# Feed-forward by whole batches, and ternary weights by sign, in a two-layer decoder kernel

## Chip, cores and metric

The kernel runs on one core of one Trainium2 chip. The metric is the device time of one execution in microseconds. Engine names are those of the profile: PE is TensorE, PEld its weight load, DVE VectorE, ACT ScalarE, POOL GpSimd, SP SyncE.

## What is computed

Two decoder layers over x of shape (8, 128, 256), 8 batches of 128 tokens: attention, a causal convolution over a context, a ternary feed-forward, a selective scan, an fp8 cross attention, a mixture of experts. The change touches the end of the convolution and the feed-forward, whose reference is, cut to what matters:

```python
def activation_quant(x):
    s = 127 / clip(max(abs(x), axis=-1), 1e-5)
    return clip(round(x * s), -128, 127) / s
def weight_quant(w):
    s = 1.0 / clip(mean(abs(w)), 1e-5)
    return clip(round(w * s), -1, 1) / s
def bit_linear(x, w): return activation_quant(x) @ weight_quant(w).T
def rms_norm(x, weight): return weight * x * rsqrt(mean(x * x) + 1e-6)

x = x + ffn(layernorm(x))
ffn(x) = bit_linear(rms_norm(silu(bit_linear(x, w_gate)) * bit_linear(x, w_up)), w_down)
```

w_gate and w_up are 1024 x 256, w_down is 256 x 1024.

## The kernel before

Each engine has one instruction stream, written out by hand stage by stage: begin, attention, convolution, feed-forward (`ffn`), scan, cross attention, experts. Semaphores alone tie the streams, and each engine runs its own in order. A batch is a tile of 128 tokens on the partitions. `link` makes DVE or POOL wait for its own last instruction.

**Convolution** (L570). A loop of 16 turns, one for each head group h. POOL forms a product (L657) that waits for PE's turn before last, PE multiplies it by a Toeplitz matrix (L717 to L719, three matmuls of 512 columns in f32), DVE multiplies the result by the query (L674) and sums it (L676). Beside this loop, ACT makes the ternary weights in three pieces of 128 x 2048: it takes the mean of their magnitude (L700), then scales and adds a constant that rounds (L706) and subtracts it (L707). In turns 10, 11 and 12, DVE clamps a rounded piece to -1..1 (L680). POOL ends with two centrings of later weights (L1329, from L660). ACT squares other weights (L1309, L1313, called from L709); the last four wait for those centrings. After the loop PE turns the results back (L731) and DVE adds them to X in four pieces (L688), then raises `x_done`.

**Feed-forward, first half** (L808 to L838). DVE takes the layer norm's statistics of X (L129, L132), ACT the roots (L162), DVE normalises (L151), takes each token's largest magnitude and the steps (L792 to L798, `steps`) and rounds a batch in two instructions (L802, L804, `front`). PE turns the batch (L919), ACT takes it from PSUM (L874), PE projects it onto gate and up (L929). The 1024 columns are done in two halves u of 512: ACT takes silu of gate (L883), DVE multiplies by up (L812, `multiply`), ACT squares and sums (L889), POOL multiplies by the norm's weight (L965), DVE takes the largest magnitude of a whole batch (L817, `biggest`). Three buffers of 512 columns (`raw`), two of silu (`sg`).

**The barrier.** Only after all eight batches does DVE add the two halves of the sums (L837), ACT takes the root of all eight (L902) and DVE the steps (L841 to L846).

**Second half** (L848 to L862, L903 to L909, L941 to L958). For each batch DVE scales (L849) and rounds (L851) into the single buffer `hq`, PE turns it in 8 pieces (L945), ACT takes it from PSUM (L906), PE projects down (L956), DVE adds to X (L861) and takes early statistics for the scan's norm (L138, L139). In its first four batches ACT also squares a piece of a later weight (L1316).

## Time and profile before

| what | value |
|---|---|
| runs | 1134.99 us median of 3 (1133.25 to 1135.4) |
| profiled execution | 1131.52 us, its span 1129.7 us, mean granted clock 0.939 |
| busy share of the span | PE 85%, DVE 70%, ACT 56%, POOL 47% |
| convolution and feed-forward | about 138 to 264 us of the span |
| chain of waits, whole span | PE 59%, DVE 17%, POOL 8%, issue 8%, ACT 7% |

In this stretch instructions take 0.2 to 5 us each and the chain changes engine every few of them, so it is the timelines of the single engines, side by side, that tell what waits for what. A row of a timeline has the start and the duration in us, the engine, the line, what it writes from what it reads, and in brackets how long the engine had been idle and which instruction ended that. "x2" means two instructions merged into one row, with their time together.

### The profile page before, as it was taken

To read this page: it belongs to the slowest core of one execution; us is meant where nothing else is said; L and a number is where in the kernel's file an instruction comes from. 1 tells how busy PE (TensorE), PEld (TensorE's weight loads), DVE (VectorE), ACT (ScalarE), POOL (GpSimd) and SP (SyncE) were. 2 spreads that over 40 slices of the span, in tenths; PEclk is the share of its full clock that TensorE was granted. 3 is DMA by queue.
4 is the path that set the end of the run, shared out by engine and by line. 5 is a ranking of instruction groups with operands and counts; after the bars stand their busy time and mean duration, and the time that the engine had idled before them with its cause. 6 is when DMAs were issued, how large, how long until landed. Compare 5 with 4: busy or idle time off the path is not lost.

```text
span 1129.7 us, 15510 instructions
## 1 busy us (share of the span) xinstructions
PE 955.3 (85%) x5202; PEld 599.6 (53%) x5218; DVE 796.1 (70%) x1319; ACT 635.8 (56%) x1522; POOL 529.4 (47%) x395
## 2 busy tenths in 40 slices
PE   5888795556456665698899999999989999999998
PEld 3666542133122223476667777777765655555554
DVE  4578799778999997778888777778785444332233
ACT  2655493477888834777886777777763232111111
POOL 4222373431699943577777665776654222000000
PEclk8899898669698897999999999999999999999999
DMA  9634001400000000000000332000031000000000
GB/s 336 284 129 150 1 1 34 141 1 1 0 1 0 0 1 0 1 1 1 1 1 1 107 77 75 2 1 1 2 99 33 1 1 1 1 19 1 1 1 19
DMA packets 24223, 43.13 MB, mean 38 GB/s; under 512 B 3600, under 2 KB 19920, under 8 KB 22608
## 3 DMA queue, kind: packets, MB, share of 16 engines
q1 hardware_dynamic: 24144, 42.14, 10.9%
q8 instruction: 42, 0.69, 0.3%
q14 instruction: 37, 0.30, 0.1%
HBM read 41.08 MB, written 1.05 MB: 37 GB/s over the span
## 4 chain that ended last, share of the span: by engine, by line
PE 59%; DVE 17%; POOL 8%; issue 8%; ACT 7%; DMA 0%; DVEq 0%; ACTq 0%; SPq 0%; POOLq 0%
PE ps L2296 13%; PE ps L2317 8%; PE ps L1868 4%; PE ps L1881 4%; PE ps L1827 4%; PE ps L1852 3%; PE ps L1835 3%; ACT ps L2141 3%; POOL wide L1371 3%; POOL arena L1214 3%; PE ps L1860 2%; PE ps L1842 2%; PE ps L2306 2%; PE ps L444 2%; PE ps L484 1%
## 5 line engine op out<-in xcount | busy, mean ns | idle before, releaser
L2335 DVE TENSOR_TENSOR arena<-arena,ps 128x512 f32<-128x512 f32 (+1 forms) x56 | 38.5, 688 | 145.8 <-ACT arena L2328 143.6
L2328 ACT ACTIVATE arena<-ps,arena 128x512 f32<-128x512 f32 (+1 forms) x56 | 38.5, 687 | 155.6 <-PE ps L2296 155.6
L2220 POOL TENSOR_TENSOR arena<-arena 128x4 f32<-128x4 f32 x96 | 98.9, 1030 | 50.6 <-DVE arena L1992 47.9
L2317 PE MATMUL ps<-wide,arena 128*128 128x256 f32 (+1 forms) x448 | 106.3, 380 | 0.0
L2141 ACT ACTIVATE ps<-ps,arena 128x128 f32<-128x128 f32 x256 | 88.4, 354 | 29.4 <-DVE arena L1971 29.2
L2133 ACT ACTIVATE arena<-ps,ones 128x512 f32<-128x512 f32 x96 | 68.2, 787 | 61.5 <-PE ps L1842 61.5
L2317 PEld LDWEIGHTS ps<-wide,arena 128*128 128x128 f32 (+1 forms) x448 | 84.7, 190 | 17.9 <-issue 1.8
L2296 PE MATMUL ps<-XT,wide 128*128 128x512 f16 (+1 forms) x384 | 93.3, 379 | 0.0
L1971 DVE TENSOR_REDUCE arena<-ps 128x4 f32<-128x512 f32 x64 | 43.7, 689 | 54.9 <-PE ps L1852 54.9
L1835 PE MATMUL ps<-wide,arena 128*128 128x512 f16 x256 | 66.8, 397 | 13.7 <-ACT arena L2133 7.2
L1852 PEld LDWEIGHTS ps<-arena 128*128 128x128 f32 x512 | 68.8, 196 | 10.3 <-ACT arena L2133 1.2
L1161 PE MATMUL ps<-arena,skip 96*128 96x512 bf16 x64 | 22.5, 438 | 59.1 <-DVE arena L1081 46.1
L1169 PE MATMUL ps<-arena,ident 128*128 128x512 f32 x128 | 69.0, 688 | 2.1 <-POOL arena L1214 1.9
L1852 PE MATMUL ps<-arena 128*128 128x128 f32 x512 | 69.1, 279 | 0.7 <-ACT arena L2133 0.7
L2210 POOL TENSOR_TENSOR arena<-arena 128x1024 bf16<-128x1024 f32 x32 | 68.3, 2134 | 0.2
L1881 PE MATMUL ps<-side,arena 128*128 128x256 f16 x512 | 67.9, 277 | 0.0
L1868 PE MATMUL ps<-arena 128*128 128x256 f32 x256 | 66.0, 382 | 0.0
L1997 DVE TENSOR_TENSOR arena<-ps,arena 128x512 f32<-128x512 f32 x96 | 60.7, 683 | 0.0
L2296 PEld LDWEIGHTS ps<-XT,wide 128*128 128x128 f16 (+1 forms) x384 | 36.9, 99 | 39.5 <-issue 2.6
L1329 POOL TENSOR_TENSOR wide<-wide,head_mean 128x1024 f32<-128x1024 f32 x12 | 23.7, 1979 | 71.3 <-DVE head_mean L1324 71.3
L1881 PEld LDWEIGHTS ps<-side,arena 128*128 128x128 bf16 x512 | 50.9, 99 | 10.3 <-issue 0.2
L2141 ACT ACTIVATION_READ_ACCUMULATOR ps<-ps,arena 128x1 f32 x256 | 56.2, 220 | 0.0
(344 smaller groups left out, 2403.3 us busy)
## 6 DMA issues: line engine op xcount, KB each, us to landing
side<-in_wproj SPq DMA_DIRECT2D x1, 4096.0 KB, 16.7
wide<-in_w_down SPq DMA_DIRECT2D x1, 3584.0 KB, 13.5
side<-in_w_gate SPq DMA_DIRECT2D x1, 3520.0 KB, 18.9
side<-in_w_up SPq DMA_DIRECT2D x1, 3520.0 KB, 12.1
wide<-in_w_gate SPq DMA_DIRECT2D x2, 1728.0 KB, 11.9
...
```

The costliest lines, as they stand in the source:

```text
L1169: last = pe.matmul(ps[:, 4 + 2 * c + j, :], k.ident[:, :], read[i % 2][:, 512 * j:512 * j + 512], start=(n == 0), stop=(n == NST - 1), ski ...
L1835: last = pe.matmul(ps[:, bank, :], x[:, c * S:(c + 1) * S], rhs, start=(i == 0), stop=(i == len(steps) - 1))
L1852: last = pe.matmul(ps[:, 4 + t, i * P:(i + 1) * P], tt[:, MAXB + h, :], tt[:, h // 2, :], start=(i == 0), stop=True, skip_group_check=True)
L1868: last = pe.matmul(ps[:, 4 + t, 2 * i * P:(2 * i + 2) * P], val[g % 2][:, 2 * t + i, :], flat(pT[t][:, 2 * i:2 * i + 2, :]), start=(i == 0 ...
L1881: last = pe.matmul(ps[:, 7, 0:D], cq[g % 2][:, i, :], w.parts(k.side, ((2 * path + half) * QH + i) * D)[part][:, 0:D], start=(half == 0 an ...
L1997: dve.tensor_tensor(qn[:, j, :].rearrange("p (h d) -> p h d", d=HD), ps[:, j, :].rearrange("p (h d) -> p h d", d=HD), rs[:, j, :].unsqueez ...
L2133: act.activation(flat(turned[g % 2][:, MAXB * j:MAXB * j + MAXB, :]), ps[:, j, :], ACT.Identity, scale=wt[:, 0:1], bias=wt[:, 1:2]).then_i ...
L2141: last = act.activation(ps[:, 4 + t, i * P:(i + 1) * P], ps[:, 4 + t, i * P:(i + 1) * P], ACT.Exp, bias=mx[:, t, i:i + 1], accum_out=den[: ...
L2210: pool.tensor_tensor(flat(cq[g % 2]), flat(cs), flat(cm[g % 2]), ALU.subtract).then_inc(cq_ready, 1)
L2220: pool.tensor_tensor(rs[:, j, :], var[:, j, :], minus_half[:, j, :], ALU.pow).then_inc(rs_ready, 1)
L2296: last = pe.matmul(self.ps[0:m, 2 * up + n % 2, :], y[:, c, :], x[:, c, :], start=(t == 0), stop=(t == len(steps) - 1))
L2317: last = pe.matmul(self.out(b), self.hid[n % 2][0:m, b * S:(b + 1) * S], self.down[0:m, j, :], start=(j == 0 and b % 2 == 0), stop=(j == M ...
```

## The change

- **Weights.** ACT's second pass over a piece is the Sign function with bias -ROUND in place of the subtraction, and writes the ternary weights at once. DVE's three clamps are gone.
- **Statistics.** Those of batches 0 and 1 are taken between the first and the second of the four additions to X.
- **Normalising.** Batches 2 to 7 are normalised by six ACT instructions (Identity with a scale and a bias for each token) in place of six on DVE.
- **First half.** One instruction takes the 1024 columns of a batch, over two PSUM banks, for silu, multiply, square and POOL's product. `raw` is two buffers in XT, `sg` a single one, `xq` two. PE projects gate, turns the next batch, then projects up.
- **Barrier.** The inverse roots are made on POOL as a power of -0.5, for batches 0 to 5 ahead of its product of batch 7, and for 6 and 7 at the end. DVE makes its steps in the same two portions.
- **Second half.** DVE rounds batches 0 and 1; ACT rounds batches 2 to 7 (`rounded`). Two of ACT's four squares of later weights are moved into the first half.

The instruction streams around the terms of the prediction, ahead of times. DVE at the end of the first half, from the last `front` on (`ps` is PSUM, XT and arena are SBUF): before,

```order
L802 TENSOR_SCALAR arena<-XN,arena 128x256 [waits ff_xq_ready]
L804 TENSOR_SCALAR arena<-arena 128x256 [waits ff_xqT_psum,dve_seq]
L812 SCALAR_TENSOR_TENSOR arena<-ps,arena 128x512 [waits ff_sq_done,ff_h_ready,ff_silu_ready,ff_up_psum] x2
L817 TENSOR_REDUCE arena<-arena 128x1 [waits ff_h_ready]
L812 SCALAR_TENSOR_TENSOR arena<-ps,arena 128x512 [waits ff_sq_done,ff_h_ready,ff_silu_ready,ff_up_psum] x2
L817 TENSOR_REDUCE arena<-arena 128x1 [waits ff_h_ready]
L812 SCALAR_TENSOR_TENSOR arena<-ps,arena 128x512 [waits ff_sq_done,ff_h_ready,ff_silu_ready,ff_up_psum]
L837 TENSOR_TENSOR arena<-arena 128x8 [waits ff_sq_done]
L817 TENSOR_REDUCE arena<-arena 128x1 [waits ff_h_ready]
L841 RECIPROCAL arena<-arena 128x8 [waits ff_rms_ready,dve_seq]
```

and with the change:

```order
L806 TENSOR_SCALAR arena<-XN,arena 128x256 [waits ff_xq_ready]
L808 TENSOR_SCALAR arena<-arena 128x256 [waits ff_xqT_psum,dve_seq]
L815 SCALAR_TENSOR_TENSOR XT<-ps,arena 128x1024 [waits ff_sq_done,ff_h_ready,ff_silu_ready,ff_up_psum]
L820 TENSOR_REDUCE arena<-arena 128x1 [waits ff_h_ready]
L815 SCALAR_TENSOR_TENSOR XT<-ps,arena 128x1024 [waits ff_sq_done,ff_h_ready,ff_silu_ready,ff_up_psum]
L820 TENSOR_REDUCE arena<-arena 128x1 [waits ff_h_ready]
L815 SCALAR_TENSOR_TENSOR XT<-ps,arena 128x1024 [waits ff_sq_done,ff_h_ready,ff_silu_ready,ff_up_psum]
L820 TENSOR_REDUCE arena<-arena 128x1 [waits ff_h_ready]
L825 TENSOR_TENSOR arena<-arena 128x6 [waits ff_rms_ready,dve_seq]
L826 TENSOR_SCALAR arena<-arena 128x6 [waits dve_seq]
```

The two halves (x2, one with the largest magnitude or a `front` in between) became one instruction of 1024 columns, `front` stays ahead of it, and the sum of the halves (L837) is gone: the steps (L825) come ahead of the last batch's largest magnitude and cover six columns.

ACT from its last squares of the first half to the root that opens the scan: before,

```order
L889 ACTIVATE arena<-arena 128x512 [waits ff_sq_done,ff_h_raw] x2
L902 ACT_TABLE_LOAD
L902 ACTIVATE arena<-arena,eps 128x8 [waits ff_ss_ready]
L906 COPY arena<-ps 128x1024 [waits ff_hqT_psum]
L1316 ACTIVATE arena,norm<-side 128x2048 [waits pw_squared,pw_proj_loaded]
L906 COPY arena<-ps 128x1024 [waits ff_hqT_psum]
L1316 ACTIVATE arena,norm<-side 128x2048 [waits pw_squared]
L906 COPY arena<-ps 128x1024 [waits ff_down_psum,ff_hqT_psum]
...
L906 COPY arena<-ps 128x1024 [waits ff_down_psum,ff_hqT_psum] x4
L162 ACTIVATE std<-mv,eps 128x8 [waits var_ready]
```

and with the change (repeats left out on both sides):

```order
L893 ACTIVATE arena<-XT 128x1024 [waits ff_sq_done,ff_h_raw] x2
L898 COPY arena<-ps 128x1024 [waits ff_hqT_psum,ff_sq_done]
L904 ACTIVATE arena<-arena 128x1024 [waits ff_hqT_psum,ff_hq_scaled]
L1349 ACTIVATE arena,norm<-side 128x2048 [waits pw_squared]
L898 COPY arena<-ps 128x1024 [waits ff_hqT_psum]
L904 ACTIVATE arena<-arena 128x1024 [waits ff_hqT_psum,ff_hq_scaled]
L1349 ACTIVATE arena,norm<-side 128x2048 [waits pw_squared]
...
L898 COPY arena<-ps 128x1024 [waits ff_down_psum,ff_hqT_psum] x2
L162 ACT_TABLE_LOAD
L162 ACTIVATE std<-mv,eps 128x8 [waits var_ready]
```

Six roundings (L904) came in between the copies (L898), two weight squares are left of four, and the table load moved from the barrier to ahead of the scan's root.

The diff, cut:

```diff
         dve.memset(k.eps[:, 0:1], LN_EPS)
         dve.memset(k.eps[:, 1:2], 1e-6)
+        dve.memset(k.eps[:, 3:4], -ROUND)
...
-    MEAN_AT, CLAMP_AT = 3, 10
+    MEAN_AT = 3
...
             dve.tensor_tensor(grid(prod[h % 2]), grid(ps[:, bank:bank + 2, :]), q, ALU.mult).then_inc(out_done, 1)
             dve.wait_ge(out_done, h + 1)
             dve.tensor_reduce(out_heads[:, :, h, :], grid(prod[h % 2]), AX.X, ALU.add).then_inc(read_out, 1)
-            if CLAMP_AT <= h < CLAMP_AT + 3:
-                n = h - CLAMP_AT
-                dve.wait_ge(rounded, n + 1)
-                dve.tensor_scalar(flat[n], raw[n], 1.0, -1.0, ALU.min, ALU.max).then_inc(k.ternary_ready, 1)
...
             last = dve.tensor_tensor(k.X[:, 2 * j:2 * j + 2, :].rearrange("p b d -> p (b d)"),
                                      k.X[:, 2 * j:2 * j + 2, :].rearrange("p b d -> p (b d)"),
                                      ps[:, j, :], ALU.add)
+            if j == 0:
+                link(last)
+                k.norm_stats(dve, link, k.X, [0, 1])
...
-            act.activation(raw[n], raw[n], ACT.Copy, bias=-ROUND).then_inc(rounded, 1)
+            act.activation(flat[n], raw[n], ACT.Sign, bias=k.eps[:, 3:4]).then_inc(k.ternary_ready, 1)
...
-    HF = FF // 2
-    sg = [A.take([HF]) for _ in range(2)]
-    raw = [A.take([HF]) for _ in range(3)]
-    xq = A.take([D], BF16)
+    sg = A.take([FF])
+    raw = [k.XT[:, c, :] for c in range(KC)]
+    xq = [A.take([D], BF16) for _ in range(2)]
     xqT = [A.take([KC, P], BF16) for _ in range(2)]
-    hq = A.take([FF], BF16)
+    hq = [A.take([FF], BF16) for _ in range(2)]
...
+    FIRST = 6
 
     lnw_loaded = k.sem("ff_lnw_loaded")
     steps_ready = k.sem("ff_steps_ready")
+    offset_ready = k.sem("ff_offset_ready")
...
+    def pair(bank):
+        return ps[:, bank:bank + 2, :].rearrange("p a n -> p (a n)")
...
-        def multiply(u):
-            b = u // 2
-            dve.wait_ge(up_psum, u + 1)
-            dve.wait_ge(silu_ready, u + 1)
-            wait(dve, sq_done, u - 2)
-            wait(dve, h_ready, u - 2)
-            dve.scalar_tensor_tensor(raw[u % 3], ps[:, 4 + u % 3, :], ustep[:, b:b + 1], sg[u % 2], ALU.mult,
+            wait(dve, xqT_psum, b - 1)
+            dve.tensor_scalar(xq[b % 2], xi, -ROUND, None, ALU.add).then_inc(xq_ready, 1)
+
+        def multiply(b):
+            dve.wait_ge(up_psum, b + 1)
+            dve.wait_ge(silu_ready, b + 1)
+            wait(dve, sq_done, b - 1)
+            wait(dve, h_ready, b - 1)
+            dve.scalar_tensor_tensor(raw[b % 2], pair(UP[b % 2]), ustep[:, b:b + 1], sg, ALU.mult,
                                      ALU.mult).then_inc(h_raw, 1)
 
...
-            dve.wait_ge(h_ready, 2 * b + 2)
-            last = dve.tensor_reduce(hmax[:, b:b + 1], h[b], AX.X, ALU.max, apply_absolute_value=True)
-            if b == B - 1:
-                link(last)
-
...
+            dve.wait_ge(h_ready, b + 1)
+            return dve.tensor_reduce(hmax[:, b:b + 1], h[b], AX.X, ALU.max, apply_absolute_value=True)
...
+        def scale(b):
+            dve.tensor_scalar(h[b], h[b], hq_scale[:, b:b + 1], ROUND, ALU.mult, ALU.add).then_inc(hq_scaled, 1)
+
+        def quantise(b):
+            scale(b)
+            dve.wait_ge(hq_scaled, b + 1)
+            dve.tensor_scalar(hq[b], h[b], -ROUND, None, ALU.add).then_inc(hq_ready, 1)
+
+        k.norm_apply(dve, link, 4, k.X, range(0, 2))
         k.norm_stats(dve, link, k.X, range(2, B))
-        k.norm_apply(dve, link, 4, k.X, range(0, 2))
         steps(0, 2)
         front(0)
         front(1)
-        k.norm_apply(dve, link, 5, k.X, range(2, B))
-        steps(2, B - 2)
+        dve.wait_ge(k.std_ready, 6)
+        link(dve.reciprocal(k.rstd[:, 2:B], k.std[:, 2:B]))
+        dve.scalar_tensor_tensor(offset[:, 2:B], k.mv[:, 2:B, 0], -1.0, k.rstd[:, 2:B], ALU.mult,
+                                 ALU.mult).then_inc(offset_ready, 1)
...
         for b in range(B):
-            multiply(2 * b)
+            if b and b + 2 < B:
+                front(b + 2)
+            multiply(b)
             if b:
-                biggest(b - 1)
-            if b + 2 < B:
-                front(b + 2)
-            multiply(2 * b + 1)
-        dve.wait_ge(sq_done, 2 * B)
-        dve.tensor_tensor(ss, ss, ss1, ALU.add).then_inc(ss_ready, 1)
-        biggest(B - 1)
-
...
-        def quantise(b):
-            link(dve.tensor_scalar(h[b], h[b], hq_scale[:, b:b + 1], ROUND, ALU.mult, ALU.add))
-            wait(dve, hqT_psum, b)
-            dve.tensor_scalar(hq, h[b], -ROUND, None, ALU.add).then_inc(hq_ready, 1)
-
+                last = biggest(b - 1)
+            if b == 0:
+                steps(2, B - 2)
+                front(2)
+        link(last)
+        down_steps(0, 0, FIRST)
         quantise(0)
         quantise(1)
+        link(biggest(B - 1))
+        scale(2)
+        down_steps(1, FIRST, B)
         for b in range(B):
-            if b + 2 < B:
-                quantise(b + 2)
+            if b + 3 < B:
+                scale(b + 3)
...
+        def silu(b):
+            act.wait_ge(gate_psum, b + 1)
+            if b in (0, 2):
+                act.wait_ge(steps_ready, 1 + b // 2)
+            wait(act, h_raw, b)
+            act.activation(sg, pair(GATE[b % 2]), ACT.Silu, scale=gstep[:, b:b + 1]).then_inc(silu_ready, 1)
...
+        def square(b):
+            act.wait_ge(h_raw, b + 1)
+            wait(act, sq_done, b)
+            act.activation(k.junk[:, 0:FF], raw[b % 2], ACT.Square, accum_out=ss[:, b:b + 1]).then_inc(sq_done, 1)
...
+        def rounded(b):
+            act.wait_ge(hq_scaled, b + 1)
+            act.wait_ge(hqT_psum, b - 1)
+            act.activation(hq[b % 2], h[b], ACT.Copy, bias=-ROUND).then_inc(hq_ready, 1)
...
         front(0)
-        front(1)
-        for u in range(2 * B):
-            silu(u)
-            if u % 2 and u // 2 + 2 < B:
-                front(u // 2 + 2)
-            if u:
-                square(u - 1)
-        square(2 * B - 1)
-        act.wait_ge(ss_ready, 1)
-        act.activation(hrms, ss, ACT.Sqrt, bias=k.eps[:, 1:2], scale=1.0 / FF).then_inc(rms_ready, 1)
...
+        act.wait_ge(offset_ready, 1)
+        for b in range(2, B):
+            act.activation(k.XN[:, b, :], k.X[:, b, :], ACT.Identity, scale=k.rstd[:, b:b + 1],
+                           bias=offset[:, b:b + 1]).then_inc(k.xn_ready, 1)
         for b in range(B):
-            act.wait_ge(hqT_psum, b + 1)
-            wait(act, down_psum, b - 1)
-            act.copy(hqT[b % 2].rearrange("p c t -> p (c t)"),
-                     ps[:, 5 * (b % 2), :].bitcast(BF16)).then_inc(hqT_ready, 1)
-            if b < 4:
-                k.proj.square(act, 12 + b, k.junk)
+            silu(b)
+            if b + 1 < B:
+                front(b + 1)
+            if b:
+                square(b - 1)
+            if b in (4, 6):
+                act.wait_ge(sq_done, b)
+                k.proj.square(act, 10 + b // 2, k.junk)
+                act.wait_ge(k.proj.squared, 11 + b // 2)
+        square(B - 1)
+        act.wait_ge(sq_done, B)
+        for b in range(B):
+            turned(b)
+            if b + 2 < B:
+                rounded(b + 2)
+            if b < 2:
+                k.proj.square(act, 14 + b, k.junk)
...
-        pe.wait_ge(k.x_done, 2)
...
+        def project(b, w, bank, done):
+            for n in range(2):
                 for c in range(KC):
-                    last = pe.matmul(ps[:, bank + u % 3, :], xqT[u // 2 % 2][:, c, :], w[:, c, HF * n:HF * n + HF],
+                    last = pe.matmul(ps[:, bank + n, :], xqT[b % 2][:, c, :], w[:, c, n * 512:n * 512 + 512],
                                      start=(c == 0), stop=(c == KC - 1))
-                last.then_inc(done, 1)
+            last.then_inc(done, 1)
...
-        front(1)
         for b in range(B):
-            project(2 * b)
-            project(2 * b + 1)
-            if b + 2 < B:
-                front(b + 2)
+            pe.wait_ge(xqT_ready, b + 1)
+            project(b, gate, GATE[b % 2], gate_psum)
+            if b == 0:
+                pe.wait_ge(k.x_done, 2)
+            if b + 1 < B:
+                front(b + 1)
+            wait(pe, h_raw, b - 1)
+            project(b, up, UP[b % 2], up_psum)
...
+            if b < 2:
+                pe.wait_ge(h_raw, B)
             wait(pe, added, b - 1)
...
+        def root(n, first, last):
+
+            some = slice(first, last)
+            pool.wait_ge(sq_done, last)
+            link(pool.tensor_scalar(hms[:, some], ss[:, some], 1.0 / FF, 1e-6, ALU.mult, ALU.add))
+            pool.tensor_tensor(hr[:, some], hms[:, some], minus_half[:, some], ALU.pow).then_inc(rms_ready, 1)
...
-        for u in range(2 * B):
-            half = slice(u % 2 * HF, (u % 2 + 1) * HF)
-            pool.wait_ge(h_raw, u + 1)
-            pool.tensor_tensor(h[u // 2][:, half], raw[u % 3], lnw[:, half], ALU.mult).then_inc(h_ready, 1)
+        for b in range(B):
+            pool.wait_ge(h_raw, b + 1)
+            pool.tensor_tensor(h[b], raw[b % 2], lnw, ALU.mult).then_inc(h_ready, 1)
+            if b == FIRST:
+                root(0, 0, FIRST)
+        root(1, FIRST, B)
```

## Rows read from the trace of the kernel before

**Rows 1.** Windows view: busy us (x count) of PE, PEld, DVE, ACT, POOL; clock, DMA.
```profile
199.60:206.00 6.40, 3.96 (x11) 1.39 (x12) 5.95 (x17) 2.12 (x4) 0.00 (x0) 0.50 1.10 350
...
250.00:264.00 14.00, 9.62 (x95) 7.31 (x93) 12.90 (x31) 10.45 (x12) 1.03 (x1) 0.98 0.01 2
264.00:280.00 16.00, 10.57 (x35) 4.51 (x36) 13.39 (x42) 11.45 (x16) 4.27 (x13) 0.94 0.00 0
```

**Rows 2.** Timeline of DVE, convolution: start us, us, what, [idle before <-releaser].
```profile
167.21 1.23 DVE L674 TENSOR_TENSOR arena<-ps,XT 128x1024 f32<-128x1024 f32 x1
...
177.80 2.63 DVE L680 TENSOR_SCALAR arena<-side 128x2048 bf16<-128x2048 f32 x1
...
186.20 1.23 DVE L674 TENSOR_TENSOR arena<-ps,XT 128x1024 f32<-128x1024 f32 x1 [0.99 <-PE ps L719]
```

**Rows 3.** Timeline of POOL, convolution: three products, then the two centrings.
```profile
164.68 1.89 POOL L657 TENSOR_TENSOR arena<-side 128x1024 f32<-128x1024 f32 x1 [0.68 <-PE ps L719]
167.25 1.89 POOL L657 TENSOR_TENSOR arena<-side 128x1024 f32<-128x1024 f32 x1 [0.68 <-PE ps L719]
...
177.46 4.73 POOL L1329 TENSOR_TENSOR wide<-wide,head_mean 128x1024 f32<-128x1024 f32 x2
```

**Rows 4.** Timeline of ACT, end of the convolution: first and last of four squares.
```profile
182.22 1.91 ACT L1313 ACTIVATE arena<-wide 128x2048 f32<-128x2048 f32 x1 [9.47 <-POOL wide L1329]
...
188.44 0.18 ACT L1313 ACTIVATION_READ_ACCUMULATOR arena<-CT 128x1 f32 x1
```

**Rows 5.** Timeline of DVE, start of the feed-forward.
```profile
193.81 2.03 DVE L129 BATCH_NORM_STATS2 stats<-X 128x6 f32<-128x256 f32 x6
...
199.21 0.29 DVE L804 TENSOR_SCALAR arena<-arena 128x256 bf16<-128x256 f32 x1
...
202.62 1.75 DVE L792 TENSOR_REDUCE arena<-XN 128x6 f32<-128x1536 f32 x1
```

**Rows 6.** Timeline of PE, eight projections at the lower clock.
```profile
207.85 3.62 PE L929 MATMUL ps<-arena 128*128 128x512 bf16 x8
```

**Rows 7.** Timeline of POOL, feed-forward multiplication, and a power in the scan.
```profile
206.20 1.26 POOL L965 TENSOR_TENSOR arena<-arena 128x512 f32<-128x512 f32 x1 [24.00 <-DVE arena L812]
...
266.13 1.91 POOL L1349 TENSOR_TENSOR total<-total,ranged 128x9 f32<-128x9 f32 x1
```

**Rows 8.** Timeline of DVE, loop over the half batches.
```profile
206.35 1.26 DVE L804 TENSOR_SCALAR arena<-arena 128x256 bf16<-128x256 f32 x1
...
223.80 0.75 DVE L812 SCALAR_TENSOR_TENSOR arena<-ps,arena 128x512 f32<-128x512 f32 x1 [1.38 <-POOL arena L965]
224.47 1.21 DVE L817 TENSOR_REDUCE arena<-arena 128x1 f32<-128x1024 f32 x1
...
228.42 0.75 DVE L812 SCALAR_TENSOR_TENSOR arena<-ps,arena 128x512 f32<-128x512 f32 x1 [1.38 <-POOL arena L965]
...
238.09 0.74 DVE L812 SCALAR_TENSOR_TENSOR arena<-ps,arena 128x512 f32<-128x512 f32 x1
```

**Rows 9.** Groups by line and form, 160 to 300 us: shapes, count | busy us, mean ns.
```profile
L906 ACT COPY arena<-ps 128x1024 bf16<-128x1024 bf16 x8 | 8.0, 1015 | 5.9 <-PE ps L945 5.9
...
L874 ACT COPY arena<-ps 128x256 bf16<-128x256 bf16 x8 | 3.0, 372 | 14.4 <-PE ps L919 14.4
...
L1122 ACT ACTIVATE arena<-ps,arena 128x1024 f32<-128x1024 f32 x2 | 2.2, 1114 | 1.4 <-PE ps L1154 1.3
...
L1365 ACT CAST wide<-arena 128x1024 f16<-128x1024 f32 x2 | 2.1, 1046 | 0.1
```

**Rows 10.** Timeline of DVE, second half: first rounded batch, last addition.
```profile
243.46 0.69 DVE L851 TENSOR_SCALAR arena<-arena 128x1024 bf16<-128x1024 f32 x1
...
263.39 0.48 DVE L861 SCALAR_TENSOR_TENSOR X<-ps,arena,X 128x256 f32<-128x256 f32 x1
```

**Rows 11.** Timeline of ACT, a table load and the root that opens the scan.
```profile
239.60 1.28 ACT L902 ACT_TABLE_LOAD   x1
...
264.70 0.30 ACT L162 ACTIVATE std<-mv,eps 128x8 f32<-128x8 f32 x1 [2.45 <-DVE mv L132]
```

75 lines of the change are left out of this document (31 added, 44 removed).

## Prediction

> **What bounds the kernel now.** I read the windows first, then the timelines of the engines side by side. The span is 1129.7 us and the change touches 164 to 264 us of it. In the windows of this stretch no engine is full: from 199.6 to 206 us PE is busy 3.96 of 6.40 us at a granted clock of 0.50 (the level of 1.2 GHz), DVE 5.95 us [rows 1]. So the time goes by hand-overs, and the timelines tell which wait ends last. The reader is to see five things in them.
>
> 1. DVE's clamps hold up the convolution. A turn of the loop takes 2.57 us, the distance of two POOL products [rows 3]. From DVE's product at 167.21 us, five turns would end at 180.1 us; the last one starts at 186.20 us [rows 2], 6.1 us late.
> 2. A clamp that meets a POOL instruction waits for it: the one at 177.80 us lasts 2.63 us because POOL's centring began at 177.46 us, and the two centrings together take 4.73 us, though one alone takes 1.9 [rows 2, 3]. The same in the feed-forward: DVE's rounding (L804) at 206.35 us takes 1.26 us where it usually takes 0.29, and ends 0.15 us after the POOL product that began at 206.20 us and took 1.26 us [rows 5, 7, 8]. The largest magnitude (L817) and the multiplication (L812) keep 1.21 and 0.75 us beside POOL [rows 8]. So two-step rounding can't run beside POOL here, the rest can.
> 3. ACT sits after four squares that wait for POOL's centrings: 182.22 to 188.62 us [rows 4].
> 4. The first half has a period of 4.62 us for a batch (223.80 to 228.42 us) and ends with the multiplication at 238.09 us, at 238.83 us [rows 8]. The barrier lasts until the first batch is rounded at 244.15 us; the last addition ends at 263.87 us [rows 10], 19.7 us later.
> 5. The root that opens the scan is 0.83 us behind that addition [rows 10, 11]. All behind it moves with it.
>
> **Convolution: without the clamps.** DVE's last product starts at 167.21 + 5 x 2.57 = 180.1 us. From there to the statistics of batches 2 to 7 it takes 186.20 to 193.81 = 7.6 us now [rows 2, 5]; the statistics of batches 0 and 1 are in that already, and only change place with additions. So DVE is ready at 187.7 us. ACT has the root to deliver: POOL's last product starts 4 turns after 164.68 us, at 175.0 us, and ends at 176.9; two centrings of 1.9 us end at 180.7; the four squares take 6.4 us [rows 3, 4], to 187.15; the root 0.3, to 187.5 us. The two meet, so ACT's queue would take the place of the clamp at once if the squares were longer. Sign for subtraction on ACT: the same 2048 columns, within the nine idle microseconds ahead of its squares [rows 4]. From 193.81 us to the first rounded batch at 199.50 us is 5.7 us [rows 5], so that batch is now ready at 193.4 us: **6.1 us early**.
>
> **Start of the loop.** Turning (0.4) and copying (0.37 [rows 9]) and four gate matmuls at 0.45 us each (eight take 3.62 [rows 6]) give 196.1 us. ACT has six Identity instructions of 256 columns first. No row shows these: the nearest is 0.37 us for a copy of 256 columns, and 1.11 us for 1024 with a scale [rows 9]; I take 0.4, with 0.3 to 0.7 as ends (-0.6 to +1.8 us in all). They end at 196.9, silu (1.11) at 198.0, up at 198.3, the multiplication (two halves of 0.75 overlapping, 1.2) at 199.5. The magnitudes and steps of six batches take 2.7 us (1.75 of it in one row [rows 5]), one `front` 0.65, and behind it PE does its turning and up: the second multiplication ends at 206.3 us.
>
> **A batch in the loop.** POOL's product becomes 1024 columns, twice 1.26 less overlap: 2.45 us [rows 7]. DVE after a multiplication takes a magnitude (1.15), and then `front` has to wait for POOL by point 2: 0.05 + 2.45 + 0.15, then 0.25 for the second rounding, then 1.2 for the next multiplication: **4.1 us**. PE at 1.2 GHz needs 3.6 + 0.4 = 4.0 [rows 6], ACT 1.1 + 0.4 + 1.2 = 2.7, with a weight square (1.91 and its readout, 2.1 [rows 4]) 4.8: under 4.1 on average. Four such batches: 222.7 us. The last two have no `front`: batch 6 follows after 3.1 us (silu, up), batch 7 waits for ACT, which has silu, copy, square, weight square and silu (1.15 + 0.4 + 1.2 + 2.1 + 1.1), then 1.2. The last multiplication ends at 229.9 us, **8.9 us early**.
>
> **The barrier.** POOL's product of batch 6 ends at 228.3 us. A power of nine columns takes 1.91 us [rows 7]; for six I take 1.5, with the instruction ahead of it 1.9 (1.4 to 2.3): 230.2. DVE has the magnitude of batch 6 at 231.1 us, so the power is covered; if it weren't, each further microsecond would count. Five small instructions 1.0, scaling and rounding 1.45, of which some 0.5 waits for POOL's product of batch 7: 234.1 us, **10.0 us early**.
>
> **Second half.** ACT has 8 copies (1.01 alone, 0.93 in a row), 6 roundings (1.05 for 1024 columns from SBUF [rows 9], 0.98 in a row) and 2 weight squares: 17.5 us. Its first copy ends at 236.1; rounding 2 waits for DVE, which rounds batch 1, takes the last magnitude and scales: 237.5 us, rounding to 238.6, square to 240.7. The rest is 7 x 0.93 + 5 x 0.98 + 2.1 = 13.5 us, to 254.2; then matmuls 1.1 and addition 0.5: 255.8 us. That is 21.7 us where it took 19.7: **2 us are given back**, since ACT is the bound now. The sum: 263.87 - 255.8 = **8.1 us**.
>
> **The scan's root.** A table load of 1.28 us [rows 11] is no longer at the barrier but ahead of this root. ACT's last copy ends at 254.2 and the root is wanted at 255.8 + 0.8 us; the load has no wait of its own, so it fits in and costs nothing. The Trainium skill, "ScalarE: Activation LUTs", section "What ACT_TABLE_LOAD costs", adds a drain of about 1.38 us to a switch; by that estimate the root would be late by 0.3 us and the gain 7.8 us. The trace has the 1.28 us and no row of the drain.
>
> SP's transfer of the later weight starts at `x_done`, near 188 us, 29 us ahead of ACT's first square of it. POOL's small work for the scan hangs on the four squares, which end earlier than before.
>
> **The number.** The profiled execution took 1131.52 us, its span 1129.7; the median of the runs is 1134.99. I take the 8.1 us off the median: **1126.9 us** (1123.4 for an execution like the profiled one).
>
> **Rivals.**
> - *Rounding isn't held by POOL.* If `front` can run beside the longer product, a batch costs DVE 1.15 + 0.65 + 1.2 = 3.0 us, and PE allows it at 2.4 GHz. Only ACT's weight squares then stretch two batches: about 4.6 us more, gain 12.7, 1122.3 us. For it: the clock was 0.98 from 250 us on [rows 1]. Against: L804 [rows 8]. Chance 0.08.
> - *ACT and PE take turns in the second half.* If each rounding, turning and copy stand one behind the other, a batch pays some 1.0 us more, six times: gain 2.1, 1132.9 us, no change. Against: the buffers are double and copy b+1 doesn't need rounding b+3. Chance 0.05; 0.02 more for work behind the scan's root that doesn't move with it.
> - *Slower: PE stays at 1.2 GHz.* The place is the second half. At 0.98 PE has 9.62 us of work for six batches [rows 1], 1.6 each; at half the clock 3.2, over ACT's 1.9: 6 x 1.3 = 7.9 us, which uses up the gain. From there each microsecond of the scan's opening counts: 10.57 us of PE work at 0.94 [rows 1], three quarters ahead of all others, 8 us more. That is 1135 - 8.1 + 7.9 + 8 = 1142.8 us. For it: 0.50 from 199.6 to 206 us. Against: PE is to be busier than it was at 0.98. Chance 0.05.
> - *The change as worked out*, 1126.9 us: its own range is 1124.5 to 1129.5 (Identity -0.6 to +1.8, power -0.1 to +0.4, a higher clock in the first half -1.5, the rest +-1). Chance 0.80.
>
> The range reaches to the first rival below, and above to a part of the second: 1122 to 1131 us. 0.2%, 2.3 us, is what a measurement here can tell. Faster 0.89, the same 0.06, slower 0.05.
>
> **What would show it.** In the trace of the changed kernel: DVE's last product near 180 us; ACT's root within 0.5 us of its last square; `front` ending just behind POOL's product; a period near 4.1 us; ACT without idle time from 239 to 254 us; the last addition 8 us before 263.87. A period near 3, or idle ACT in the second half, would prove the step named wrong.

## The result, and the profile after

The change made the kernel 0.7% faster: **1125.11 us** (median of 4 runs, 1124.94 to 1126.66) against 1135.2 us for the kernel before, measured beside it (4 runs, 1133.25 to 1136.82). The ratio is 0.9926, with an interval of 0.9910 to 0.9943: 10.0 us in medians. The prediction was 1126.9 us, within 1122 to 1131. The profiled execution took 1126.66 us, the longest of the four, its span 1124.9. So the time was within the range. Whether the steps were right is read stage by stage, since up to the end of the feed-forward the traces give a smaller gain than the medians: 6.8 us.

The times of the two traces can't be laid side by side as they are. DVE's product of turn 10 of the convolution, the last point ahead of the first edit, began at 167.21 us before [rows 2] and at 168.29 us after. I take 1.08 us off all times of after and call that *aligned*.

**DVE in the changed kernel** (timeline as in [rows 2, 5, 8, 10]: start, duration, instruction, idle time before it and its releaser):

```profile
168.29 1.22 DVE L674 TENSOR_TENSOR arena<-ps,XT 128x1024 f32<-128x1024 f32 x1
...
181.16 1.22 DVE L674 TENSOR_TENSOR arena<-ps,XT 128x1024 f32<-128x1024 f32 x1
...
188.31 0.17 DVE L149 RECIPROCAL rstd<-std 128x2 f32<-128x2 f32 x1 [0.39 <-ACT std L162]
...
202.11 0.85 DVE L797 TENSOR_SCALAR arena<-arena 128x6 f32<-128x6 f32 x1
...
206.82 1.28 DVE L815 SCALAR_TENSOR_TENSOR XT<-ps,arena 128x1024 f32<-128x1024 f32 x1 [1.48 <-PE ps L947]
208.02 1.21 DVE L820 TENSOR_REDUCE arena<-arena 128x1 f32<-128x1024 f32 x1
209.14 1.54 DVE L806 TENSOR_SCALAR arena<-XN,arena 128x256 f32<-128x256 f32 x1
...
210.93 1.28 DVE L815 SCALAR_TENSOR_TENSOR XT<-ps,arena 128x1024 f32<-128x1024 f32 x1
...
232.75 1.28 DVE L825 TENSOR_TENSOR arena<-arena 128x6 f32<-128x6 f32 x1
234.07 0.17 DVE L826 TENSOR_SCALAR arena<-arena 128x6 f32<-128x6 f32 x1
```

What the reader is to see: the last product of the convolution is exactly five turns of 2.57 us behind turn 10, 181.16 us, aligned 180.08. In the loop the multiplications (L815) stand at 206.82 and 210.93 us, 4.1 us apart, and so do the next three. The first half of a rounding (L806, 256 columns) takes 1.54 us, and two tiny steps on 128 x 6 numbers take 0.85 us (202.11) and 1.28 us (232.75), though the one behind the second takes 0.17 (234.07). The reason stands in **POOL's rows**:

```profile
177.91 3.75 POOL L1362 TENSOR_TENSOR wide<-wide,head_mean 128x1024 f32<-128x1024 f32 x2
...
200.59 2.35 POOL L995 TENSOR_TENSOR arena<-XT,arena 128x1024 f32<-128x1024 f32 x1 [18.89 <-DVE XT L815]
208.18 2.36 POOL L995 TENSOR_TENSOR arena<-XT,arena 128x1024 f32<-128x1024 f32 x1 [5.24 <-DVE XT L815]
...
229.92 1.35 POOL L989 TENSOR_TENSOR arena<-arena 128x6 f32<-128x6 f32 x1
231.67 2.34 POOL L995 TENSOR_TENSOR arena<-XT,arena 128x1024 f32<-128x1024 f32 x1 [0.40 <-DVE XT L815]
```

The two centrings take 3.75 us and no longer 4.73 [rows 3]. The products of 200.59, 208.18 and 231.67 us end at 202.94, 210.54 and 234.01 us; the three long DVE rows end at 202.96, 210.68 and 234.03 us. Each ends with the product, whatever its own size. The trace of the kernel before had such a small step too: its L837, which adds the two halves of the sums of squares (128 x 8 numbers), stood beside a POOL product that ended at 240.17 us.

```profile
239.62 0.57 DVE L837 TENSOR_TENSOR arena<-arena 128x8 f32<-128x8 f32 x1 [0.79 <-ACT arena L889]
```

It took 0.57 us and ended at 240.19, while a product of the same 128 x 8 numbers without POOL beside it took 0.17 us (L842, 241.69 us). The prediction doesn't use this row.

**ACT**, from the convolution's squares to the scan's root (compare [rows 4, 11]):

```profile
187.90 0.19 ACT L1346 ACTIVATION_READ_ACCUMULATOR arena<-CT 128x1 f32 x1
188.00 0.28 ACT L162 ACTIVATE std<-mv,eps 128x2 f32<-128x2 f32 x1
...
192.11 1.28 ACT L908 ACT_TABLE_LOAD   x1
193.40 0.20 ACT L908 ACTIVATE warm<-eps 128x1 f32<-128x1 f32 x1
...
194.96 3.06 ACT L912 ACTIVATE XN<-X,arena,rstd 128x256 f32<-128x256 f32 x6
...
237.50 1.01 ACT L898 COPY arena<-ps 128x1024 bf16<-128x1024 bf16 x1 [4.73 <-PE ps L966]
239.66 1.06 ACT L904 ACTIVATE arena<-arena 128x1024 bf16<-128x1024 f32 x1 [1.15 <-DVE arena L833]
...
252.64 1.01 ACT L898 COPY arena<-ps 128x1024 bf16<-128x1024 bf16 x1 [0.59 <-PE ps L966]
...
256.44 1.28 ACT L162 ACT_TABLE_LOAD   x1
259.01 0.30 ACT L162 ACTIVATE std<-mv,eps 128x8 f32<-128x8 f32 x1 [1.28 <-DVE mv L132]
```

ACT's root (188.00) starts when its squares end, and DVE waits 0.39 us for it (188.31 in DVE's rows): ACT's queue and DVE meet, as predicted. ACT is idle for 4.73 us ahead of its first copy of the second half (237.50), and afterwards only for 1.15 and 0.59 us. The table load (256.44) is over 1.28 us before the root begins, whose row names DVE as its releaser: it is hidden.

**Windows**, the second half up to 252 us (columns as in [rows 1]):

```profile
237.00:252.00 15.00, 11.62 (x73) 8.36 (x72) 9.13 (x22) 13.34 (x14) 0.55 (x2) 0.50 0.00 0
```

ACT is busy 13.34 of 15 us: it is the fullest engine of the second half. Before, DVE was (12.90 of 14) [rows 1]. PE's clock is 0.50 there, the level of 1.2 GHz.

### The profile page after: what moved, and what is told of

Its sections match the earlier page's. It is cut to its first block, busy times and chain, and to the rows that moved or that the text cites. A ratio compares the mean times of both kernels' runs of the same rounds, so it can differ in the third digit from the quotient of the medians.

```text
span 1124.9 us, 15437 instructions
## 1 busy us (share of the span) xinstructions
PE 959.0 (85%) x5202; PEld 602.3 (54%) x5218; DVE 789.0 (70%) x1301; ACT 640.8 (57%) x1509; POOL 528.6 (47%) x392
## 4 chain that ended last, share of the span: by engine, by line
PE 59%; DVE 15%; POOL 9%; issue 8%; ACT 8%; DMA 0%; DVEq 0%; ACTq 0%; SPq 0%; POOLq 0%
PE ps L2329 13%; PE ps L2350 9%; PE ps L1901 4%; PE ps L1914 4%; PE ps L1860 4%; PE ps L1868 3%; PE ps L1885 3%; ACT ps L2174 3%; POOL wide L1404 3%; POOL arena L1247 3%; PE ps L1893 2%; PE ps L1875 2%; PE ps L2339 2%; PE ps L445 2%; PE ps L485 1%
## 5 line engine op out<-in xcount | busy, mean ns | idle before, releaser
L1202 PE MATMUL ps<-arena,ident 128*128 128x512 f32 x128 | 73.0, 725 | 1.9 <-POOL arena L1247 1.9
L1885 PEld LDWEIGHTS ps<-arena 128*128 128x128 f32 x512 | 68.5, 195 | 10.3 <-ACT arena L2166 1.2
L2243 POOL TENSOR_TENSOR arena<-arena 128x1024 bf16<-128x1024 f32 x32 | 68.2, 2132 | 0.2
L2030 DVE TENSOR_TENSOR arena<-ps,arena 128x512 f32<-128x512 f32 x96 | 60.7, 685 | 0.0
L1362 POOL TENSOR_TENSOR wide<-wide,head_mean 128x1024 f32<-128x1024 f32 x12 | 22.7, 1896 | 71.6 <-DVE head_mean L1357 71.6
```

The source lines that it names most:

```text
L1202: last = pe.matmul(ps[:, 4 + 2 * c + j, :], k.ident[:, :], read[i % 2][:, 512 * j:512 * j + 512], start=(n == 0), stop=(n == NST - 1), ski ...
L1885: last = pe.matmul(ps[:, 4 + t, i * P:(i + 1) * P], tt[:, MAXB + h, :], tt[:, h // 2, :], start=(i == 0), stop=True, skip_group_check=True)
L2030: dve.tensor_tensor(qn[:, j, :].rearrange("p (h d) -> p h d", d=HD), ps[:, j, :].rearrange("p (h d) -> p h d", d=HD), rs[:, j, :].unsqueez ...
L2243: pool.tensor_tensor(flat(cq[g % 2]), flat(cs), flat(cm[g % 2]), ALU.subtract).then_inc(cq_ready, 1)
```

## The experiments

They ran in three sets, the first two on one chip and the third on another, each beside the kernel before, whose median was 1133.29 us in the first set (25 runs), 1132.53 in the second (11) and 1132.52 in the third (11). The third set has the last three runs: both edits to the second half, the product behind the rounding, and the squares in the gap, again. The table counts from DVE's product of turn 10 (the first row shown of DVE above) to the ends of four DVE instructions in each trace: the rounding of the first batch, the last multiplication, the rounding of the first batch for down, and the last addition to X. "Second half" is the last column of these less the one before it, taken before rounding. The ratios are to the kernel before of the same set, with a 95% interval.

| kernel | first batch rounded | last multiplication | rounded for down | last addition | second half | ratio to before |
|---|---|---|---|---|---|---|
| before | 32.3 | 71.6 | 76.9 | 96.7 | 19.7 | |
| before again | 32.3 | 71.7 | 77.0 | 96.7 | 19.7 | 0.9988 [0.9971, 1.0005] |
| sign alone | 26.2 | 65.5 | 70.8 | 90.6 | 19.7 | 0.9968 [0.9955, 0.9982] |
| feed-forward alone | 31.1 | 68.5 | 73.3 | 94.4 | 21.2 | 0.9993 [0.9977, 1.0010] |
| the change | 25.6 | 63.3 | 68.0 | 89.9 | 21.9 | 0.9926 [0.9910, 0.9943] |
| the change again | 25.8 | 63.5 | 68.2 | 89.7 | 21.5 | 0.9941 [0.9928, 0.9954] |
| squares in the gap | 25.6 | 63.3 | 68.0 | 85.3 | 17.3 | 0.9914 [0.9899, 0.9930] |
| squares in the gap, again | 25.8 | 63.5 | 68.2 | 85.5 | 17.3 | 0.9904 [0.9888, 0.9920] |
| rounding of x on ACT | 25.6 | 61.9 | 66.9 | 87.9 | 21.0 | 0.9922 [0.9897, 0.9946] |
| DVE rounds in the second half | 25.8 | 63.5 | 68.2 | 88.2 | 20.0 | 0.9931 [0.9914, 0.9948] |
| rounding on ACT and squares moved | 25.6 | 60.7 | 66.9 | 86.2 | 19.3 | 0.9932 [0.9918, 0.9947] |
| squares in the gap, and DVE rounds | 25.6 | 63.3 | 68.0 | 87.4 | 19.4 | 0.9929 [0.9909, 0.9949] |
| product behind the rounding | 25.6 | 63.3 | 66.9 | 90.4 | 23.5 | 0.9940 [0.9923, 0.9957] |

Where kernels share the code, these columns agree within 0.4 us. The rest of an execution doesn't: from the last addition to DVE's last instruction the traces differ by 3.7 us, from 862.6 (before again) to 866.3 us (sign alone). Two traces of one kernel differ there by 0.6 (before), 1.0 (the change) and 1.4 us (squares in the gap), so whether the remainder belongs to the kernels or to chance isn't shown. The kernel before has 863.2 and 862.6, the change 864.1 and 863.0: up to 1.5 us of the gain may be lost behind the feed-forward. That is why each verdict below rests on the columns first and on the time second.

### Nothing changed: how far a time carries

> The kernel before, unchanged, once more. It measures what two executions of one kernel differ by, and where. The two profiled executions differ by 4.8 us of span, the medians by 10.1 us. If that is the spread of single executions (first theory), this trace comes out nearer the median of 1135 us, with the last addition of the feed-forward later than 263.87 us or the scan longer, at a lower granted clock there. If the change really brings 10 us by a place I haven't seen (rival), this trace repeats 1131.5 us.

Measured: 1132.41 us, ratio 0.9988, an interval that holds 1. The profiled execution took 1131.01 us, so the trace repeated the first one, which had been named as the rival's sign. The 10 us were still not real in full, as 25 runs of this kernel with a median of 1133.29 us show (see the change again, below). The stage is the same to 0.1 us, and behind it the same code takes different times. Here are PE's first matmuls of the scan in the two executions of this kernel, before:

```profile
265.74 2.70 PE L177 MATMUL ps<-ident,XN 128*128 128x128 f32 x16 [2.39 <-DVE XN L151]
268.28 3.60 PE L1147 MATMUL ps<-XT,arena 128*96 128x512 f32 x8
```

and before again:

```profile
265.89 3.06 PE L177 MATMUL ps<-ident,XN 128*128 128x128 f32 x16 [2.39 <-DVE XN L151]
268.74 4.85 PE L1147 MATMUL ps<-XT,arena 128*96 128x512 f32 x8
```

The same sixteen and eight matmuls take 2.70 and 3.60 us in one and 3.06 and 4.85 us in the other, where the granted clock from 265.7 to 272 us was 1.00 and 0.73. At this one place the lower clock costs 1.6 us, as much as an edit moves. By the end it had come back elsewhere: the second trace's rest is the shorter one by 0.6 us.

### Each half of the change by itself

The first puts only Sign into the kernel before:

```diff
-            act.activation(raw[n], raw[n], ACT.Copy, bias=-ROUND).then_inc(rounded, 1)
+            act.activation(flat[n], raw[n], ACT.Sign, bias=k.eps[:, 3:4]).then_inc(k.ternary_ready, 1)
```

with the three clamps on DVE gone. The second is the changed kernel with ACT's subtraction and DVE's clamps put back.

> The kernel before with the sign in place of the clamps, and nothing else. First theory: the clamps are nearly the whole gain, 6.1 us at the start of the feed-forward, and the rest of the feed-forward moves with it unchanged (period 4.6 us, 19.7 us for the second half): 6 us faster than before. Rival: ACT's squares hold the root back (they end near 187.2 us), so that only 3 to 4 us arrive, and it is the whole-batch feed-forward that brings the rest.

> The changed kernel with the subtraction and the three clamps put back. First theory: the new feed-forward gains 3 to 4 us up to the barrier and gives most of it back in the second half, so alone it is worth 0 to 2 us. Rival: it is worth 4 us or more, since the clamps only hid behind ACT's queue.

Measured: Sign alone takes 6.1 us off the first rounded batch and keeps them up to the last addition (96.7 to 90.6 us). So ACT's squares didn't hold the root back, as the rival had it. In the time only 3.2 us of that show (1130.12 against 1133.29 us, ratio 0.9968); its profiled execution has the longest rest of all behind the last addition, 866.3 us. The feed-forward alone brings 2.2 us at the last addition, and 0.7 us in the time, which can't be told from nothing. In the times the two halves thus add up to 3.9 us and the whole change brings 6.7 (below); at the last addition they add up to more than the change. The longest rests of all traces are those of the two halves (866.3 and 865.9 us), and why isn't shown. The DVE rows of the feed-forward alone show the clamps and POOL in each other's way, as in the kernel before [rows 2, 3]:

```profile
179.86 2.63 DVE L681 TENSOR_SCALAR arena<-side 128x2048 bf16<-128x2048 f32 x1
...
187.86 1.23 DVE L675 TENSOR_TENSOR arena<-ps,XT 128x1024 f32<-128x1024 f32 x1 [0.59 <-PE ps L723]
```

The feed-forward's 2.2 us are made of a gain and a loss: 1.2 at the first rounded batch, 1.9 in the first half, 0.6 at the barrier, and 1.5 back in the second half. Up to the end of the barrier that is 3.7 us, as expected, and less than half of it is given back, where most was expected. Of the 1.2 us, 0.4 are there at the last product of the convolution, ahead of the edit (18.6 us behind turn 10 and no longer 19.0). The rest is that of the statistics of batches 0 and 1, taken between the additions: additions and these statistics end 3.5 us after the first addition began, in place of 4.4. The two effects add up to 8.3 us and the change has 6.8: together they give up 0.6 us ahead of the first rounded batch (the 0.4 of the convolution, which go with the clamps, and DVE's wait of 0.39 us for ACT's root), 0.3 in the first half and 0.7 in the second, where the clock of PE was 0.50 and with the feed-forward alone 0.65. In the second trace of the change, with a clock of 0.61, it is 0.3 in the second half.

### The change again

> The changed kernel, unchanged, in one session with the next three. The profiles say that the feed-forward's last addition comes 6 to 7 us earlier (beside the same turn of the convolution), and that what follows differs from execution to execution by up to 3.7 us. First theory: over many executions the change is worth 7 us, ratio 0.993 to 0.995, and the 10 us of the first measurement were a slow set of executions of the kernel before. Rival (sign and feed-forward help each other beyond their sum, which was 4 us in the timed runs): ratio 0.992 or less again.

Measured: 1125.87 us, ratio 0.9941, as the first theory has it. The intervals of the two measurements overlap, and 0.9928 to 0.9943 lies in both: a gain of 6.5 to 8.2 us. The second trace gives 7.0 us at the last addition. So the 10.0 us in medians of the first measurement were in part chance in the few runs of the kernel before (1135.2 us in 4 runs, 1132.5 and 1133.3 in the sets with more).

### What holds the loop: `front` on ACT

DVE's rounding of x in the loop is moved to ACT; all else stays:

```diff
-            if b and b + 2 < B:
-                front(b + 2)
             multiply(b)
...
+            if b and b + 2 < B:
+                round_x(b + 2)
```

> The changed kernel with the rounding of the input for batches 3 to 7 on ACT in place of DVE (two Copy instructions of 256 columns for each). First theory (DVE's rounding waits for POOL's product and so sets the period of 4.1 us): the period falls to 3.0 to 3.6 us, the bound being ACT's 3.6 us or PE, and the last multiplication comes 1 to 2 us earlier, less what ACT's weight squares then cost. Rival (the period is set by something else, PE at 1.2 GHz or silu): it stays at 4.1 us or grows.

```profile
212.31 1.28 DVE L815 SCALAR_TENSOR_TENSOR XT<-ps,arena 128x1024 f32<-128x1024 f32 x1 [0.75 <-ACT arena L886]
...
215.47 1.28 DVE L815 SCALAR_TENSOR_TENSOR XT<-ps,arena 128x1024 f32<-128x1024 f32 x1 [0.75 <-ACT arena L886]
...
220.81 1.28 DVE L815 SCALAR_TENSOR_TENSOR XT<-ps,arena 128x1024 f32<-128x1024 f32 x1 [2.93 <-ACT arena L886]
```

Measured: where no weight square stands in ACT's queue the period falls from 4.10 to 3.16 us (212.31 to 215.47), while POOL's product keeps its 2.35 us. So it was `front` on DVE that set 4.1 us. The run takes its work and its wait away together; which of them counts stands in the rows of the change, where the first instruction of `front` (L806) takes 1.54 us beside the product and 0.35 away from it (203.94 us). The next limit is ACT: each multiplication waits for silu (`<-ACT arena L886`), 0.75 us in a plain batch and 2.93 us in one with a weight square. That makes one period 5.34 us, and so the last multiplication comes only 1.4 us sooner. Both lie within what was expected. The time is 1125.40 against 1125.87 us, no difference that can be told.

### What holds the second half: three edits

ACT's two weight squares of the second half, moved ahead of its first copy:

```diff
+        for i in (14, 15):
+            k.proj.square(act, i, k.junk)
         for b in range(B):
             turned(b)
             if b + 2 < B:
                 rounded(b + 2)
-            if b < 2:
-                k.proj.square(act, 14 + b, k.junk)
```

> The changed kernel with ACT's last two weight squares (4.2 us) put ahead of its first copy of the second half, where it waits 4.7 us for the first rounded batch. First theory (ACT's queue is the bound of the second half): the span from the first rounded batch to the last addition falls from 21.9 us by 3 to 4 us, and the kernel is 3 us faster than the changed one. Rival (PE at 1.2 GHz is the bound, 2.9 us for a batch): it falls by under 1.5 us.

```profile
232.79 1.91 ACT L1349 ACTIVATE arena<-side 128x2048 bf16<-128x2048 f32 x1
...
234.82 1.91 ACT L1349 ACTIVATE arena<-side 128x2048 bf16<-128x2048 f32 x1
...
237.44 1.01 ACT L898 COPY arena<-ps 128x1024 bf16<-128x1024 bf16 x1 [0.61 <-PE ps L966]
...
240.61 0.99 ACT L898 COPY arena<-ps 128x1024 bf16<-128x1024 bf16 x1
241.50 1.06 ACT L904 ACTIVATE arena<-arena 128x1024 bf16<-128x1024 f32 x1
242.46 1.00 ACT L898 COPY arena<-ps 128x1024 bf16<-128x1024 bf16 x1
```

Measured: both squares fit into the idle time (behind them ACT still waits 0.61 us for the first copy, which starts when it did: 237.44 and 237.50 us). Rounding and copy then alternate without a gap, 1.85 us for a batch, and the second half takes 17.3 us: 4.6 us less than in the first trace of the change and 4.2 less than in the second, more than the 3 to 4 expected. PE's clock rose with the edit: from 242 to 252 us it was 0.98, in the two traces of the change 0.50 and 0.66. The clock can't be the main cause, since ACT waited for PE only 0.59 us in that stretch of the change. The time is 1123.07 us, 2.0 and 2.8 below the two medians of the change, where 3 were expected.

The next edit leaves the squares and has DVE round all eight batches (`quantise` in place of `scale` on DVE and `rounded` on ACT).

> The changed kernel with all eight roundings of the second half on DVE, as before the change. First theory (ACT's queue, six roundings longer, gives back 2 us): from the first rounded batch to the last addition it takes 19.5 to 20.5 us in place of 21.9, and the kernel is 1.5 us faster than the changed one. Rival (the first batches are slow because PE is at 1.2 GHz and ACT has its weight squares, the roundings don't matter): 21.5 us or more.

Measured: a second half of 20.0 us, within the expected range, and 1124.27 us, which can't be told from the change. It is half a relief: in the first batches ACT still has copy and square, 2.8 us a batch; in the last ones DVE is the bound. The third takes both edits at once.

> The changed kernel with both edits to the second half: ACT's two weight squares ahead of its first copy, and DVE rounds all batches. The squares alone gave a second half (first rounded batch to last addition) of 17.3 us, DVE's rounding alone 19.95, the changed kernel 21.5 to 21.9. Theory: with ACT relieved twice DVE is the bound, which has some 2.4 us of work for a batch there (scale 0.75, rounding 0.69, addition, early statistics): about 19.5 us as with DVE's rounding alone, so 2 us slower than the squares alone. Rival: ACT is still the bound in both, and the gains add: 15.4 us, and a time 2 us below that of the squares alone.

```profile
241.00 0.45 DVE L871 SCALAR_TENSOR_TENSOR X<-ps,arena,X 128x256 f32<-128x256 f32 x1
241.37 0.74 DVE L833 TENSOR_SCALAR arena<-arena 128x1024 f32<-128x1024 f32 x1
242.14 0.69 DVE L839 TENSOR_SCALAR arena<-arena 128x1024 bf16<-128x1024 f32 x1
...
243.31 0.45 DVE L871 SCALAR_TENSOR_TENSOR X<-ps,arena,X 128x256 f32<-128x256 f32 x1
```

Measured: 19.4 us, as expected. DVE works without a gap, from addition to addition 2.31 us (241.00 to 243.31), over the 1.85 us that ACT needs with the roundings in its queue. The gains don't add; each edit only hands the bound over. The median is 1125.58 us, 4.1 above the squares in the gap of the same set (next), where 2 were expected. The profiled execution took 1119.59 us, the shortest of all: its convolution reached turn 10 already at 163.44 us, and that is no merit of the edit.

> The same kernel as the squares in the gap, again, for the size of its gain. In its first run it took 1123.07 us (0.9914 of the kernel before), the changed kernel 1125.1 and 1125.9. Theory: its second half is 17.3 us again, 4.3 less than the changed kernel's, and the time lies 2 to 4.5 us below it, a ratio of 0.990 to 0.992. Rival: the gain lies within what the clock of the later stages adds or takes from run to run, and the ratio comes out at 0.993 to 0.995.

Measured: 17.3 us again, 1121.47 us, ratio 0.9904, within the expected range. It is the best version of this study: its two medians lie 2.8 and 4.4 us below the change as it was measured in the second set. The change itself wasn't run in the third; the ratios, 0.9904 [0.9888, 0.9920] and 0.9941 [0.9928, 0.9954], don't overlap.

### Both at once, and less

Rounding of x on ACT, one weight square less in the loop, two in the gap and one in the second half:

> The changed kernel with rounding of the input on ACT (as in the run above), and three weight squares moved: two into ACT's idle time ahead of its first copy, one behind its first rounding. First theory: the last multiplication comes 2 to 4 us earlier (no square ahead of silu of batch 7, shorter period) and the second half takes some 19 us, so the last addition is 5 to 7 us earlier than in the changed kernel and the kernel 5 us faster. Rival (PE's clock falls for want of work and takes it back): under 3 us.

Measured: 1124.88 us, 1.0 us below the change and 1.8 to 3.4 above the squares in the gap alone. That is far from the 5 us expected. The last multiplication is 2.6 us sooner than in the first trace of the change, but the first batch is rounded for down only 1.1 us sooner, and the last addition comes 3.7 sooner where 5 to 7 were expected. DVE's rows at the barrier say where 1.5 us went:

```profile
231.79 2.24 DVE L825 TENSOR_TENSOR arena<-arena 128x6 f32<-128x6 f32 x1 [0.57 <-POOL arena L997]
```

DVE is done early and waits 0.57 us for POOL's power. In this time POOL's product of batch 7 (231.67 us, 2.34 us) has begun, and the first small step takes 2.24 us: it is held for the whole product. So 0.57 us of waiting and 0.96 of a longer hold took back 1.5 of the 2.6 us that the loop had gained. The time came out under the 3 us that the rival named, but its reason, a falling clock, isn't shown: from 242 to 252 us the clock was 0.83, higher than in either trace of the change.

### The small steps and POOL's product

POOL's product of batch 7 is held back until DVE has rounded batch 0:

```diff
             pool.wait_ge(h_raw, b + 1)
+            if b > FIRST:
+                pool.wait_ge(hq_ready, 1)
```

> The changed kernel, with POOL's product of batch 7 held back until DVE has rounded batch 0. Theory (a DVE instruction with two SBUF inputs is held by a POOL product, however small it is): DVE's first small step (128x6) falls from 1.28 to 0.17 us, and the first batch is rounded 1.1 us sooner after the last multiplication (3.6 us in place of 4.7). In exchange the scaling of batch 1 or the largest magnitude of batch 7 waits, so that the second half is 1 us longer or more, and the time is the same or up to 2 us longer. Rival: the 1.28 us belong to the step itself or to POOL's power; then it stays near 1.28 us and the first batch is rounded no sooner.

```profile
232.63 1.21 DVE L820 TENSOR_REDUCE arena<-arena 128x1 f32<-128x1024 f32 x1
233.88 0.17 DVE L825 TENSOR_TENSOR arena<-arena 128x6 f32<-128x6 f32 x1
...
235.63 0.69 DVE L838 TENSOR_SCALAR arena<-arena 128x1024 bf16<-128x1024 f32 x1
...
237.02 2.72 DVE L838 TENSOR_SCALAR arena<-arena 128x1024 bf16<-128x1024 f32 x1
```

and POOL's product:

```profile
236.47 2.72 POOL L997 TENSOR_TENSOR arena<-XT,arena 128x1024 f32<-128x1024 f32 x1 [4.06 <-DVE arena L838]
```

Measured: L825 falls from 1.28 to 0.17 us (233.88), and the first batch is rounded 3.6 us behind the last multiplication in place of 4.7: the hold was the product's, neither the step's own nor the power's. The price came as expected: the rounding of batch 1 (237.02) now takes 2.72 us beside the late product, the second half 23.5 us, 1.6 to 2.0 longer, and the time is 1126.00 us, which can't be told from the change.

## Why the prediction was right

**Convolution.** The clamps were what held it, and for the time worked out. The last product came 0.02 us from the forecast (aligned 180.08, 180.1 foreseen), the centrings lost the hold by the clamp, ACT's root met DVE, and Sign alone shows 6.1 us, the number in the text. One term was put at nothing: "the statistics of batches 0 and 1 [...] only change place with additions". In their new place they save time, and the first batch was rounded at aligned 192.8 us, forecast 193.4: 6.7 us early and not 6.1.

**Start of the loop.** The six Identity take 3.06 us, 0.5 each where 0.4 was taken, within the ends of 0.3 to 0.7; they end at aligned 196.9 us as foreseen. But the second multiplication ended at aligned 207.0 us, 0.7 later than forecast. The step that failed is "the magnitudes and steps of six batches take 2.7 us": they took 3.3, since the small step at 202.11 us took 0.85 us and not 0.17 while POOL's first product was not over. In this stream `front` of batch 2 stands behind it, and PE turns batch 2 ahead of the up matmuls of batch 1, for which the multiplication waited (1.48 us in its row).

**A batch in the loop.** 4.1 us predicted, 4.10 measured. The rounding on ACT shows that `front` set it, and the rows that most of `front` was its wait for POOL. The last multiplication ended at aligned 230.5 us (229.9 foreseen), with the 0.7 us from above still in it.

**The barrier.** The power of six columns takes 1.35 us (1.5 taken), and ends at aligned 230.2 us as forecast. The first batch was rounded at aligned 235.2 us, forecast 234.1. The step that failed: "scaling and rounding 1.45, of which some 0.5 waits for POOL's product of batch 7". That there is such a wait was right; its place and its size were wrong. The product held the step ahead of the scaling, and for 1.1 us: I had looked only at instructions that are long by themselves, and not at L837 of the trace before. The run with the product held back confirms the 1.1 us.

**Second half.** 21.9 and 21.5 us, 21.7 predicted, ACT the bound, and 2 us given back: right. ACT's rows show it (one wait for PE of 0.59 us from 242 us on), and the squares in the gap confirm it and show also that the loss was not necessary.

**The scan's root.** The load is hidden. The Trainium skill, "ScalarE: Activation LUTs", section "What ACT_TABLE_LOAD costs", adds a drain of about 1.38 us to a load at every switch to a different set, by which the root would have been ready 0.3 us late in the forecast. The rows show none. In the changed kernel the instruction after the load of 192.11 us begins at 193.40, 0.01 us behind its end. In the kernel before, the barrier's load began at 239.60 us, 0.01 us behind ACT's last readout, and the root 0.02 us behind the load [rows 11]:

```profile
240.90 0.30 ACT L902 ACTIVATE arena<-arena,eps 128x8 f32<-128x8 f32 x1
```

So the sum for the last addition was 8.1 us and the traces show 6.8 and 7.0. Of the difference of 1.3 us, 0.7 and 0.6 belong to the two small steps behind a POOL product. What is left cancels, and that is luck: the statistics gave 0.6 us that the sum didn't count, and the six Identity took 0.7 more than the 2.4 taken. The predicted time was nearer than this, 1.8 us from the first median and 1.0 from the second, and the gain in medians was larger than in the traces (10.0 and 6.7 us against 6.8 and 7.0): the median of before, 1134.99, lay some 2 us above that of the sets with more runs. So the closeness of the time is luck in part: a base some 2 us too high and a gain some 1.2 too large, by the traces, partly cancel. The forecast of 1123.4 us for an execution like the profiled one shows the error bare. The two profiled executions of the change took 1126.66 and 1124.70 us. Of the 8.1 us of span the first one shows only 4.8: 6.8 in the stage, less 1.1 that it lost ahead of turn 10 and 0.9 behind the last addition.

**The rivals.** *Rounding isn't held by POOL*: refuted, in the loop L806 ends 0.14 us behind the product in each of the four batches that have both. *ACT and PE take turns*: refuted, from 242 us ACT has one gap, of 0.59 us. *Slower, since PE stays at 1.2 GHz*: its condition came true, its price did not. PE's rows in the second half of the changed kernel:

```profile
248.99 1.06 PE L966 MATMUL ps<-ident_bf,arena 128*128 128x128 bf16 x8
249.84 1.91 PE L979 MATMUL ps<-arena 128*128 128x256 bf16 x8
251.55 1.06 PE L966 MATMUL ps<-ident_bf,arena 128*128 128x128 bf16 x8
...
253.37 0.61 PE L966 MATMUL ps<-ident_bf,arena 128*128 128x128 bf16 x8
253.81 1.04 PE L979 MATMUL ps<-arena 128*128 128x256 bf16 x8
```

Until 252.4 us turning takes 1.06 us and down 1.9, afterwards 0.61 and 1.04. Once, from 248.99 to 251.55 us, PE is the bound with 2.56 us for a batch; otherwise ACT's batches of 3.75 us with a weight square cover it. In the change again, whose clock was 0.61 in this stretch, the second half was 0.4 us shorter. The rival charged six batches at PE's rate of 3.2 us; only one paid it, at 2.56. The second part of its price, 8 us at the scan's opening, didn't arise either: from 252 to 275 us the clock was 0.95 on average.
